# Coupling stage of a frequency-domain solver: where the base of the third block is added, and its banks

## The reference

```python
vfft = jnp.fft.rfft2(weight, s=(n, n), norm='ortho')     # 128 x 127 at each of 34 x 18 frequencies
wfft = vH @ vfft + eps * I                               # per frequency
ortho = I - 2.0 * (vfft @ jnp.linalg.solve(wfft, vH))
zfft = ortho @ xfft                                      # xfft: rfft2 of the normalised, padded x
out = x + irfft2(zfft)[..., 1:-1, 1:-1] + bias
```

## Time and profile before

| | us |
|---|---|
| median of 3 runs | 4109.44 |
| lowest and highest run | 4084.66 and 4148.07 |
| the profiled execution | 4130.5 |
| its span | 4128.3 |
| TensorE busy, of the span | 2959.8 |
| VectorE busy | 2165.5 |
| ScalarE busy | 1163.9 |

### The profile page before, as it was taken

The page is one execution under the profiler, slowest core; times in us unless marked ns, Lnnn a source line. Parts: engine busy times, 40 slices in busy tenths (PEclk is TensorE's granted clock), DMA queues, the critical chain, the costliest instruction groups (busy, mean ns, idle before and its releaser), DMA issues. The chain is left out here.

```text
span 4128.3 us, 97147 instructions
## 1 busy us (share of the span) xinstructions
PE 2959.8 (72%) x42317; PEld 2379.4 (58%) x42317; DVE 2165.5 (52%) x4711; ACT 1163.9 (28%) x2659; POOL 716.1 (17%) x1331
## 2 busy tenths in 40 slices
PE   6875376332988888888877877866697666647677
PEld 3375334222776666667666665655576555547677
DVE  4184327777786667765687576566504672002122
ACT  1332122111443443443423232212243222211111
POOL 2400000000221122211223223111222222200000
PEclk6597788666998999987877576556797566657667
DMA  5443501000222123211311112010232011232332
GB/s 164 80 94 70 92 27 24 1 1 1 56 49 45 41 54 68 41 37 44 69 48 48 34 41 68 25 32 28 54 78 61 28 51 49 71 95 103 110 118 85
DMA packets 286453, 235.84 MB, mean 57 GB/s; under 512 B 216696, under 2 KB 228600, under 8 KB 285192
## 3 DMA queue, kind: packets, MB, share of 16 engines
q1 hardware_dynamic: 254784, 146.84, 14.9%
q0 software_dynamic: 31248, 82.79, 7.0%
HBM read 126.15 MB, written 103.28 MB: 56 GB/s over the span
## 5 line engine op out<-in xcount | busy, mean ns | idle before, releaser
L1274 DVE SCALAR_TENSOR_TENSOR arena<-arena,psum 128x448 f32<-128x448 f32 (+1 forms) x640 | 403.6, 693 | 673.3 <-PE psum L910 673.3
L1238 DVE TENSOR_TENSOR arena<-arena 128x192 f32<-128x192 f32 (+7 forms) x720 | 456.6, 634 | 24.8
L889 PEld LDWEIGHTS psum<-arena 32*32 32x32 f32 x9280 | 186.0, 132 | 466.0 <-issue 459.1
L889 PE MATMUL psum<-arena 32*32 32x64 f32 x9280 | 216.5, 257 | 327.6 <-issue 220.8
L910 PE MATMUL psum<-arena 32*128 32x64 f32 x9280 | 360.8, 310 | 93.7 <-DVE arena L1274 92.8
L910 PEld LDWEIGHTS psum<-arena 32*128 32x128 f32 x9280 | 339.2, 223 | 135.2 <-issue 116.1
L1233 DVE TENSOR_TENSOR arena<-arena 128x960 f32<-128x960 f32 (+2 forms) x600 | 408.4, 714 | 12.4
L777 POOL COPY arena<-arena 128x464 f32<-128x464 f32 x160 | 85.6, 581 | 1580.1 <-ACT arena L1076 1580.1
L1371 PE MATMUL psum<-arena 68*128 68x64 f32 x1152 | 184.6, 338 | 185.2 <-DMA arena<-yhat 125.0
L1371 PEld LDWEIGHTS psum<-arena 68*128 68x128 f32 x1152 | 181.2, 252 | 186.8 <-DMA arena<-yhat 126.1
L858 PE MATMUL psum<-arena 128*32 128x256 f32 (+1 forms) x1744 | 186.6, 492 | 119.9 <-DMA arena<-plain 90.2
(11 more groups left out here) (125 smaller groups left out, 5584.4 us busy)
## 6 DMA issues: line engine op xcount, KB each, us to landing
kept<-arena POOLq DMA_DIRECT2D x145, 256.0 KB, 2.8
arena<-kept SPq DMA_DIRECT2D x145, 256.0 KB, 2.9
xhat<-arena SPq DMA_DIRECT2D x32, 580.0 KB, 13.0
yhat<-arena POOLq DMA_DIRECT2D x290, 64.0 KB, 2.4
arena<-yhat SPq DMA_DIRECT2D x64, 272.0 KB
arena<-x SPq DMA_DIRECT2D x8, 2048.0 KB, 9.6
arena<-x SPq DMA_DIRECT2D x32, 512.0 KB, 14.9
out<-arena POOLq DMA_DIRECT2D x32, 512.0 KB, 6.3
```

The lines of the kernel that those rows point to most:

```text
L889: ins = pe.matmul(psum[0][h, L * t:L * t + L], ce[h, sj % NCE, slot + t, :], M[h, home(q) + t, c, :], start=True, stop=True)
L1238: link(dve.tensor_tensor(rest, rest, pr[:, :, h], op))
L1274: ins = dve.scalar_tensor_tensor(old, old, K["mask"][:, piv:piv + 1], psum[2 + c][:, 0:L * n].rearrange("p (t n) -> p t n", n=L), ALU.mult ...
```

## The change

The third block's base is no longer added by the eight products with the identity (L972). Instead, ScalarE's `copy_s` leaves out its first copy, and a new VectorE function `add_base` waits for `copy_s`, adds `base` to the block in the banks and writes the sum into M, counting `s_based`. VectorE calls it inside `eliminate`: `mids_beside` lists the quads that run beside a factorisation, and the addition of the i-th stands ahead of pivot 2 + i; of 15, the last stands behind `place`. For group c's 29 quads, whose results the factorisation needs, all additions stand ahead of `take`. Odd quads use the banks 1 and 2, even ones 4 and 5, so `schur(m)` waits for the copies and the addition of quad m - 2; `solve_b` moves to bank 3. The table load, the sweep's `settle` and the gathering after a coupling stage now wait for `s_based`.

```diff
+        def schur_banks(m):
+            first = (4, 1)[m % 2]
+            pair = psum_all[:, 512 * first:512 * (first + 2)].rearrange("p (b n) -> p b n", b=2)
+            return pair[:, :, 0:10 * NB].rearrange("p b (f n) -> p b f n", f=2)
...
-                        load_tables(schur_loads, n, t_schur, 2, {"mid": "s_done"}, "t_schur_in")
+                        load_tables(schur_loads, n, t_schur, 2, {"mid": "s_based"}, "t_schur_in")
...
                         if done["mid"]:
                             pe.wait_ge(S["s_copied"], done["mid"])
+                            pe.wait_ge(S["s_based"], done["mid"])
...
-                            ins = pe.matmul(psum[2][:, 3 * NB * f:3 * NB * f + 3 * NB],
+                            ins = pe.matmul(psum[3][:, 3 * NB * f:3 * NB * f + 3 * NB],
...
-                        if m:
-                            pe.wait_ge(S["s_copied"], m)
-                        banks = psum_all[:, 4 * 512:6 * 512].rearrange("p (b n) -> p b n", b=2)[:, :, 0:10 * NB].rearrange(
-                            "p b (f n) -> p b f n", f=2)
+                        if m >= 2:
+                            pe.wait_ge(S["s_copied"], m - 1)
+                            pe.wait_ge(S["s_based"], m - 1)
+                        banks = schur_banks(m)
...
-                        for p in range(LB):
-                            for b in range(2):
-                                k = 2 * b % ks
-                                pe.matmul(banks[quadrant(p), b, :, 0:L], K["ident"][:, quadrant(p)], base[:, k:k + 2, :],
-                                          start=False, stop=False)
...
                         act.wait_ge(S["s_done"], m + 1)
...
-                        act.copy(two(M[:, home(mid_quads[m]), :, :]), banks[:, :, :, 0:L])
...
-                                act.wait_ge(S["s_copied"], before("mid", at))
+                                act.wait_ge(S["s_based"], before("mid", at))
...
-                    def eliminate(n):
+                    def eliminate(n, beside):
                         lanes = list(R.ap[0])
                         for j in range(B):
+                            if 2 <= j < 2 + len(beside):
+                                add_base(beside[j - 2])
...
+                    def mids_beside(g, k):
+                        at = [job[0:3] for job in jobs].index(("sweep", g, k))
+                        first = max([n for n in range(at) if jobs[n][0] == "sweep"], default=-1) + 1
+                        return [m for job in jobs[first:at] if job[0] == "mid" for m in range(job[3], job[4])]
+
+                    def add_base(m):
+                        q = mid_quads[m]
+                        ks = len({FREQ[f][1] for f in range(QUAD * q, QUAD * q + QUAD)})
+                        base = t_schur[1]
+                        if ks == QUAD:
+                            base = base.rearrange("p (b f) n -> p b f n", b=2)
+                        else:
+                            base = spread(base[:, 0:ks, :], 1, 2)
+                        dve.wait_ge(S["s_copied"], m + 1)
+                        dve.tensor_tensor(M[:, home(q), :, :].rearrange("p (b f) n -> p b f n", b=2), schur_banks(m)[:, :, :, 0:L],
+                                          base, ALU.add).then_inc(S["s_based"], 1)
...
                         n = len(GROUPS[g])
+                        beside = mids_beside(g, k)
+                        if beside and mid_quads[beside[0]] in quads_of(g):
+                            for m in beside:
+                                add_base(m)
+                            beside = []
...
-                        eliminate(n)
+                        eliminate(n, beside)
                         scale(n)
                         for t in range(n):
                             place(set_job_at[g, k, GROUPS[g][t]], t)
+                        for m in beside[B - 2:]:
+                            add_base(m)
```

More of the change, by code:

```diff
@@ L705, in build @@
                  "u_done", "u_copied", "upd_done", "added", "upd_copied",
-                 "j_turned", "ju_copied", "b_done", "b_copied", "p_copied", "turned", "j_copied", "t_done", "t_copied", "s_done", "s_copied",
+                 "j_turned", "ju_copied", "b_done", "b_copied", "p_copied", "turned", "j_copied", "t_done", "t_copied", "s_done", "s_copied", "s_based",
                  "q_turned", "q_copied", "q_beside", "jq_copied", "z_done", "z_copied", "y_done", "y_copied"]
@@ L1111, in copy_t @@
                             act.wait_ge(S[f"part_stored{q % 2}"], 16 * (m // 2))
-                        src = psum[2][:, 0:QUAD * 3 * NB].rearrange("p (f n) -> p f n", f=QUAD)
+                        src = psum[3][:, 0:QUAD * 3 * NB].rearrange("p (f n) -> p f n", f=QUAD)
                         act.copy(work[:, m % 2, :, 0:L], src[:, :, 0:L])
```

## The result

The changed kernel takes 4166.65 us (median of 4 runs, 4146.9 to 4174.31), beside 4100.27 for the kernel before (4 runs): a ratio of 1.0167, 95% interval 1.0107 to 1.0228. Ratios are taken from the fast runs of both kernels alone and so differ a little from the quotient of the medians beside them. The forecast was +0.8%, 4143 us with a range of 4095 to 4200: right in direction and range, low in size. The profiled execution of the changed kernel took 4146.9 us, the shortest of its four runs.

A forecast was written before the change was run, and what follows sets the result against it. A coupling stage belongs to TensorE, with VectorE nearly as long in the first eight of nine. Terms +84 - 38 - 12 = +34 us on 4109.4 gave 4143 us, +0.8%, 8 in 10 within 4095 to 4200.

The forecast's parts named there:

- The products' price: Third block of each quad: dropping eight base products saves 0.46 us, period 4.72; 51.5 us in stages 4 to 11.
- The coupling: Stages 4 to 11: additions in VectorE's queue tie the elimination to the quads' pace; quads' end to first update, +84 us.
- The walk through stage 4: Stage 4, quad by quad: quad 13 ends at 1112.4, first update comes at 1130.8, 5.7 us later than before.
- The tail: VectorE's pivot 15, scaling and placing at a coupling stage's end: 13.2 us, after quad 13's addition.
- The 0.8 us for TensorE's wait: Stages 4, 5 and 9, over quads 4 to 7: third block waits for quad i - 2's addition, 0.8 us once.
- The additions: VectorE's additions, one per quad, 256 columns with one input in PSUM: 0.42 us each, 145 of them.
- The table: Third block's table request waits for the addition: 5.7 us late in stage 6, 1.2 in 8, 4.3 in 11; together +11.
- the sweep's start: Stages 4 to 11, to the first update: 4.0 us from the tail's end (14 quads), 6.0 from the fifteenth addition (15).
- The clock did fall: Rival: slow TensorE stretches inside the quads; one of 10 us per stage gives 40 more, 4183, two 4223; chance 0.12.
- VectorE's own pace: Rival: in coupling stages VectorE, not the quads, sets pivot 15 from a period of 4.4 down; 4090 us; chance 0.14.
- ScalarE did not hold the period: Rival denied here: ScalarE or the semaphores hold the quads' period at 5.18; +94 us, 4203; chance 0.07.
- Full-clock sweeps: Rival: after the pauses all sweeps run at full clock, 35 us instead of 38 on average; 4112 us; chance 0.09.

The follow-up runs named there:

- e3_wait: Changed kernel with base products and first copy put back, VectorE's addition left out, its wait for the copies kept: 4252.99 us, ratio 1.0371 to before.
- e4_late: Changed kernel with the additions of quads 12, 13 (and 14) moved behind scale, between the two placings and behind them: ratio 1.0107 to before.
- e6_tables: Changed kernel with two buffers for the base table, so the third block's table is asked for when the products are done: ratio 1.0091 to before.
- second trace: Trace of the changed kernel timed again without edit, over more rounds (the second timing): 4162.21 us against 4111.58 before, ratio 1.0139.
- e9_warm_full: Changed kernel with 11 or 12 unread products in TensorE's pause ahead of the sweeps of stages 4 to 11: ratio 1.0056 to before.
- e1_banks: Kernel before with only the two pairs of banks (and bank 3 for the solve): ratio 1.0012 to before.
- e8_split: Changed kernel with only 63 quads' additions by VectorE, the others keeping base products and ScalarE's copy: 4082.71 us against 4111.58 before, ratio 0.9931.
- e10_late_tables: Changed kernel with the edits of e4_late and e6_tables together: 4119.33 us, ratio 1.002 to before.
- e5_pool: Changed kernel with ScalarE copying the block into M as before and GpSimd, not VectorE, adding the base there: 4142.7 us, ratio 1.0099 to before.
- e7_warm: Changed kernel with nine unread products in TensorE's pause ahead of each sweep in stages 4 to 11: ratio 1.0141 to before.

## Why the prediction was right or wrong

**The products' price: right.** Forecast 0.46 us a quad and a period of 4.72; measured 4.72. The union of their records, 0.67, was not what came back; the step to the next products was. The last coupling stage gained 12.4 (forecast 11.8). Quad 13 of the eight stages ended 39.8 us earlier in sum, counted from the take (forecast 38).

**The coupling: right in mechanism.** The walk through stage 4 had quad 13's end at 1112.4 counted from the old take; with the new take 0.8 us earlier it would be 1111.6, and it was 1111.16. The tail was forecast at 13.2 and took 13.1. e3_wait shows that waits without work cost 104 us, e4_late that their place decides. I had VectorE waiting from about pivot 12 on; in the stages without a table load it waited from pivot 13. The 0.8 us for TensorE's wait on the addition of the quad two before did not come in stages 4 and 9, where all periods but the last are 4.72, and came as 0.7 in stage 5.

**The additions: right**, 0.425 us each (forecast 0.42).

**The table: right.** The end of quad 4's products in stage 6, the request and the quad that waited:

```profile
1340.56 0.41 PE L982 MATMUL psum<-arena 128*32 128x64 f32 x16
...
1347.98 0.36 SPq L727 DMA_DIRECT2D arena<-terms  x1
...
1353.45 0.71 PE L955 MATMUL psum<-arena 128*128 128x96 f32 x2 [11.61 <-DMA arena<-xhat]
```

The request went out 7.0 us after the quad's end (forecast 5.7), the period grew by 6.1. e6_tables gives 11 us back for all of them (forecast 11). By stage it is 6.6, 0.1 and 3.8 in stages 6, 8 and 11 (forecast 5.7, 1.2 and 4.3).

**The term that was too small: the sweep's start.** The forecast added 84 us from the quads' ends to the first updates; it was 55.6 + 39.8 = 95 in the first trace and 92 in the second. For a stage of 15 the forecast took 6.0 us from the addition to the first update, from the earlier trace rows, where TensorE went from the last quad to the sweep without a pause; for one of 14 it took 4.0. The end of stage 5 in the changed kernel:

```profile
1246.26 0.41 PE L982 MATMUL psum<-arena 128*32 128x64 f32 x16
...
1247.00 0.27 ACT L1122 COPY arena<-psum 128x128 f32<-128x128 f32 x1
...
1257.10 0.42 DVE L1294 TENSOR_TENSOR arena<-psum,arena 128x256 f32<-128x256 f32 x1
...
1257.85 1.93 PE L894 MATMUL psum<-arena 32*32 32x64 f32 x64 [11.18 <-DVE arena L1294]
...
1264.12 3.69 PE L915 MATMUL psum<-arena 32*128 32x64 f32 x64
...
1267.88 0.75 DVE L1275 SCALAR_TENSOR_TENSOR arena<-arena,psum 128x512 f32<-128x512 f32 x1 [10.35 <-PE psum L915]
```

Before, the first update's products there were:

```profile
1250.69 2.02 PE L910 MATMUL psum<-arena 32*128 32x64 f32 x64
```

The first apply's 64 records took 1.93 us where they had taken 1.10, those of the first update's products 3.69 for 2.02, and from the placing's end at 1256.96 it was 10.9 us, 4.4 more than forecast. Stages 5 and 9 lost 9 us by it, the four stages of 14, at 4.9 us on average, 3.5. In the second trace the clock had risen before those products (2.01 us), and it was 5 and 2 us. The text said itself that TensorE now pauses before each sweep, and left it in the 4.0; it had the 1.93 beside the 1.10 and did not carry it into the 6.0. The pause was 10.2 to 11.2 us and not about 15. e9_warm_full shows that the slow start is the clock: 15.8 us come back when the pause is filled, more than the forecast lacked, since its 4.0 held part of them.

So the traces show +43 and +44, not +34. The times say +57 (42 to 72 by the interval of the second timing). The 13 us between are open. The sums give the measured ratio to within 8 us in e1_banks, e6_tables, e8_split, e9_warm_full and e10_late_tables; in e3_wait and e5_pool they fall short by 47 and 29 us, beyond their intervals. So there is a loss that the sums do not hold, in some kernels at least, and no trace shows where. That the total came within the range was in part luck: a term was short by some 10 us, and this unplaced part is not in the forecast at all.

**The rivals.** The clock did fall, but in the sweep's start and not inside the quads (0.96 to 0.97 in the stages without a table load). VectorE's own pace did not come about, since the period stayed over 4.4. ScalarE did not hold the period. Full-clock sweeps did not come: the eight took 309.6 us in the first trace and 304.4 in the second, 305.8 before.

## What to carry to other kernels

A wait in an in-order queue costs everything behind it: before putting another engine's result between the steps of a long chain, lay the two engines' times side by side to the last step, and keep late arrivals out of the chain's tail. Removing work from the engine that ends last helps only up to the time of the engine beside it, so the work is to be split to where both end together, as e8_split comes near to doing. When a pause is moved in front of a burst of matmuls, price the burst at the lower clock.

## What was not expected of the hardware

An addition of GpSimd in SBUF (0.82 us) lengthened VectorE's factorisation by 0.9 us each (e5_pool), so that moving the work off VectorE cost VectorE about twice the addition's own 0.42 us. And nine products that left TensorE idle for 2.3 to 3.4 us before the sweep held its clock in some stages and not in others: the first apply took between 1.09 and 1.93 us. With 11 and 12 that left 0.6 to 0.9 it took 1.09 or 1.10 in all eight (e7_warm, e9_warm_full). And a sweep can run at the lower level from end to end with TensorE busy 45.7 of 49 us (e3_wait, stages 7 and 11).
